# Scattering a sorted group three groups of gathers later, from three row buffers

## What is computed

```python
msgs = x[src]                                   # a row for each edge
dense = zeros((n + 1, 5, d)).at[dst_s, slot].set(msgs[order])
filled = dense[:, :4] + (~mask)[..., None] * (W @ blank + b)
srt = jnp.sort(filled, axis=1)                  # 4 values for each node and feature
out = jnp.einsum('nmd,m->nd', srt, cw) + cb
h = batch_norm(a * x + out[:-1], g, be)         # needs mean and variance over all nodes
x = x + h
```

## Time and profile before

| | us |
|---|---|
| median of three runs | 5594.01 |
| lowest, highest | 5585.44, 5599.05 |
| profiled execution, all of it | 5594.62 |
| its span, from first to last instruction | 5592.8 |

### The profile page before, as it was taken

The page is one execution under the profiler, slowest core; times in us unless marked ns, Lnnn a source line. Parts: engine busy times, 40 slices in busy tenths (PEclk is TensorE's granted clock), DMA queues, the critical chain, the costliest instruction groups (busy, mean ns, idle before and its releaser), DMA issues. The chain is left out here.

```text
span 5592.8 us, 61115 instructions
## 1 busy us (share of the span) xinstructions
PE 4068.6 (73%) x14728; PEld 2251.4 (40%) x14728; DVE 3828.8 (68%) x7518; ACT 2782.3 (50%) x5374; POOL 3409.5 (61%) x3399
## 2 busy tenths in 40 slices
PE   6755446700444775554879999999999989995597
PEld 4432223300222334442546555655565545553343
DVE  7876664588666358884768776877787778762276
ACT  6862222212222236664778645864685468544433
POOL 7757777776777727776777402730371057677677
PEclk9987668855766888887999999999999999997799
DMA  5643225876111589883768645864585467875455
GB/s 181 230 177 102 93 97 201 289 260 233 47 46 46 182 274 269 263 258 121 226 208 267 225 159 165 262 207 148 188 256 200 139 218 254 260 225 151 137 174 166
DMA packets 628092, 1062.85 MB, mean 190 GB/s; under 512 B 105048, under 2 KB 258158, under 8 KB 627740
## 3 DMA queue, kind: packets, MB, share of 16 engines
q1 hardware_dynamic: 498972, 818.46, 44.8%
q0 software_dynamic: 100544, 163.41, 10.5%
q10 hardware_dynamic: 28224, 77.08, 3.5%
HBM read 599.34 MB, written 464.81 MB: 190 GB/s over the span
## 5 line engine op out<-in xcount | busy, mean ns | idle before, releaser
L1831 POOL DMA_INDIRECT r_G<-msg_tab,srow x784 | 739.9, 944 | 1107.3 <-issue 1103.1
L827 PE MATMUL l_ps<-cv_V,cv_cwi 128*128 128x448 f32 x896 | 476.0, 699 | 815.6 <-DVEq L814 815.6
L827 PEld LDWEIGHTS l_ps<-cv_V,cv_cwi 128*128 128x128 f32 x896 | 218.8, 252 | 1073.4 <-issue 552.6
L1221 POOL DMA_INDIRECT x_tab<-a_r,node_pos x392 | 379.7, 969 | 223.6 <-issue 114.0
L2080 DVE TENSOR_TENSOR agg<-r_psS,agg 128x128 f32 x980 | 281.7, 287 | 289.8 <-PE r_psS L1938 216.7
L696 POOL DMA_INDIRECT o_tab<-cv_ob,put_idx x392 | 387.9, 989 | 148.7 <-issue 113.9
L1912 PE MATMUL r_psR<-r_hin,whh 128*128 128x512 f32 x882 | 453.4, 596 | 0.9 <-ACT r_ohn L2011 0.9
L688 POOL DMA_INDIRECT cv_M<-h_tab,gat_src x392 | 373.9, 954 | 119.4 <-issue 119.1
L1863 PEld LDWEIGHTS r_psM<-wmsg,r_hnew 128*128 128x128 f32 x2744 | 360.5, 192 | 169.7 <-issue 140.2
L1938 PE MATMUL r_psS<-r_sel,r_G 128*128 128x128 f32 x1960 | 293.8, 297 | 136.0 <-DMA r_G<-msg_tab,srow 135.0
L1863 PE MATMUL r_psM<-wmsg,r_hnew 128*128 128x128 f32 x2744 | 362.8, 275 | 3.9 <-DVE r_hnew L2144 3.9
(11 more groups left out here) (287 smaller groups left out, 10768.5 us busy)
## 6 DMA issues: line engine op xcount, KB each, us to landing
r_hin<-ht_tab SPq DMA_DIRECT2D x441, 256.0 KB
msg_tab<-r_m SPq DMA_DIRECT2D x392, 256.0 KB
ht_tab<-r_hnew SPq DMA_DIRECT2D x343, 256.0 KB
o_tab<-o_blank SPq DMA_DIRECT2D x98, 512.0 KB, 4.9
st_h<-h_tab SPq DMA_DIRECT2D x98, 512.0 KB, 3.7
st_o<-o_tab SPq DMA_DIRECT2D x98, 512.0 KB, 4.7
r_oin<-ht_tab SPq DMA_DIRECT2D x161, 256.0 KB
i_x<-x_tab SPq DMA_DIRECT2D x49, 528.0 KB
```

The source lines that it names most:

```text
L827: ins = nc.tensor.matmul(psO[:, h, 0:HW], cwi[m][:], V[i % 2][m][:, HW * h:HW * (h + 1)], start=m == 0, stop=m == 3)
L1221: pool.indirect_dma_start(x2_tab, bass.IndirectOffsetOnAxis(ap=node_pos[:, j:j + 1], axis=0), rb[i % RR][:, t, :], None).then_inc(s_out[i ...
L1831: pool.indirect_dma_start(G[g % GR][:, q, :], None, msg_tab[s % 3] if s else first_tab, bass.IndirectOffsetOnAxis(ap=at, axis=0)).then_inc ...
```

## The change

GpSimd's order in the sort of both layers becomes gather(0) to gather(3), scatter(0), gather(4), scatter(1), ... gather(27), scatter(24), scatter(25), scatter(26), scatter(27). The number of row buffers `ob` and of the semaphores that go with them becomes OR = 3, so that ACT's `rows(i)` waits for the scatter of group i - 3. SP's wait for the end of all scatters has three semaphores. The number of instructions that move data stays.

```diff
--- before.py
+++ after.py
@@ -36,6 +36,7 @@
 SR = 4
 AR = 3
 RR = 4
+OR = 3
 SW = P
 IDW = D + 4
 LNEPS = 1e-5
@@ -643,14 +644,14 @@
             s_srt = stage_sem(n + "sorted")
             s_mix = stage_sem(n + "mixed")
             s_o = stage_sem(n + "rows")
-            s_sc = [stage_sem(n + "put0"), stage_sem(n + "put1")]
+            s_sc = [stage_sem(f"{n}put{i}") for i in range(OR)]
             M0 = sb(n + "M_first", [P, 3, D], F32, c)
             M = [sb(f"{n}M{i}", [P, JC + 1, D], F32, c) for i in range(CR)]
             low = [sb(f"{n}low{i}", [P, JC + 2, D], F32, c) for i in range(2)]
             high = [sb(f"{n}high{i}", [P, JC + 2, D], F32, c) for i in range(2)]
             A = sb(n + "A", [P, JC, D], F32, c)
             V = [[sb(f"{n}V{i}{m}", [P, JC * D], F32, c) for m in range(4)] for i in range(2)]
-            ob = [sb(f"{n}ob{i}", [P, JC, D], F32, c) for i in range(2)]
+            ob = [sb(f"{n}ob{i}", [P, JC, D], F32, c) for i in range(OR)]
             cwi = [sb(f"{n}cwi{m}", [P, P], F32, c) for m in range(4)]
             HW = JC * D // 2
             psS, psL, psH, psW = banks
@@ -675,8 +676,8 @@
                 sp.wait_ge(s_fill, 16 * NCH)
 
             def scattered(sp):
-                for par in range(2):
-                    sp.wait_ge(s_sc[par], 16 * JC * (NC // 2))
+                for q in range(OR):
+                    sp.wait_ge(s_sc[q], 16 * JC * ((NC - 1 - q) // OR + 1))
 
             def gpsimd(pool):
                 def gather(i):
@@ -695,18 +696,18 @@
                         j = JC * i + q
                         pool.indirect_dma_start(o_tab[layer],
                                                 bass.IndirectOffsetOnAxis(ap=put_idx[:, j:j + 1], axis=0),
-                                                ob[i % 2][:, q, :], None, bounds_check=N - 1, oob_is_err=False
-                                                ).then_inc(s_sc[i % 2], 16)
+                                                ob[i % OR][:, q, :], None, bounds_check=N - 1, oob_is_err=False
+                                                ).then_inc(s_sc[i % OR], 16)
 
                 for q in range(3):
                     pool.indirect_dma_start(M0[:, q, :], None, h_tab[layer],
                                             bass.IndirectOffsetOnAxis(ap=gat_src[:, q:q + 1], axis=0)
                                             ).then_inc(s_m0, 16)
-                for i in range(NC + 2):
+                for i in range(NC + OR):
                     if i < NC:
                         gather(i)
-                    if i >= 2:
-                        scatter(i - 2)
+                    if i >= OR:
+                        scatter(i - OR)
 
             def scalar(act):
                 bl = blank_p[layer][:].unsqueeze(1)
@@ -746,9 +747,9 @@
 
                 def rows(i):
                     act.wait_ge(s_mix, i + 1)
-                    if i >= 2:
-                        act.wait_ge(s_sc[i % 2], 16 * JC * (i // 2))
-                    nc.scalar.activation(ob[i % 2][:].rearrange("p j f -> p (j f)").rearrange("p (h n) -> p h n", n=HW),
+                    if i >= OR:
+                        act.wait_ge(s_sc[i % OR], 16 * JC * (i // OR))
+                    nc.scalar.activation(ob[i % OR][:].rearrange("p j f -> p (j f)").rearrange("p (h n) -> p h n", n=HW),
                                          psO[:, :, 0:HW], ACT.Identity, bias=cbb[layer][:, 0:1]).then_inc(s_o, 1)
 
                 blank_first(-1)
```

## The result

| | before | after |
|---|---|---|
| median, us (7 runs each) | 5596.28 | 5566.32 |
| lowest, highest | 5585.44, 5599.15 | 5557.86, 5572.98 |
| profiled execution's span | 5592.8 | 5567.4 |
| ratio, 95% interval | | 0.9946 [0.9936, 0.9956] |

The change is worth 30 us of 5596, with an interval of 25 to 36. Forecast were 5568 and 26.1 less. It is clear of the 0.3% that one can tell from no change.

A forecast was written before the change was run, and what follows sets the result against it. GpSimd's issuing of gathers and scatters was taken as the bound, with idle holes at both ends of each sort. 8.80 + 5.48 + 6.09 + 5.71 = 26.1 us less gave a median of 5568, range 5557 to 5583.

The forecast's parts named there:

- (1): Sort heads: a fourth group of gathers fills the wait before the first scatter; gain 8.80 us layer 0, 6.09 layer 1.
- (2): Sort tails: three groups of scatters cover the wait for the last rows; gain 5.48 us layer 0, 5.71 layer 1.
- (3): Sort's middle: same instructions, scatters one group later, 0 us; ACT's wait for a scatter's landing has 10 us of cover.
- (4): Small parts: SP's third semaphore wait and one more semaphore cleared per stage; under 0.2 us, taken as 0.
- (5): Moved gathers beside DVE's sorting might take longer, costing up to 10 us; taken as 0.
- rival C: Holes filled, but something that doesn't move sets the end of the sort stages: no gain, 5594 us; chance 0.10.
- Rival D: Recurrent stage, 2913 to 5050: PE's granted clock falls; gain gone from 0.979 downward, 5635 us at 0.96; chance 0.05.
- Rival B: Only the heads' gain comes, last rows being late or gathers stretched: 14.9 us, time 5579; chance 0.09.

The follow-up runs named there:

- head alone: Changed kernel with four groups of gathers before the first scatter, but its last gathers left where they stood before the change: 5576.25 us, ratio 0.9955 to the kernel before.
- buffers alone: Changed kernel with three row buffers and semaphores kept, but scatters two groups behind the gathers as before: 5594.04 us, ratio 0.9993 to the kernel before.
- the change again: The changed kernel unaltered, rerun beside the kernel before on the same chip: 5563.97 us, ratio 0.9941.
- tail alone: Changed kernel with the old order up to group 25, then the last two gathers together and four scatters behind: 5587.89 us, ratio 0.9977 to the kernel before.
- lag one: Changed kernel with scatters one group behind the gathers, three buffers: 6535 us (before 6451), ratio 1.037, and 6446 us (before 6453) in three sets.
- deeper lags: Changed kernel with lag three and two buffers (ratios 1.013, 1.004), lag four and three buffers (1.0045), or unaltered (1.0059), against the kernel before.

## Why the prediction was right

**(1) The head.** Forecast a hole of 3.6 us in layer 0 and none in layer 1, gain 8.80 + 6.09. Measured 3.61 and 0.30; head alone shortened the sorts by 9.04 and 6.33.

**(2) The tail.** Forecast 5.48 + 5.71, rows ready 3.3 and 3.1 us early. Measured waits of 0.30, and the tail alone gave 5.67 and 5.26. In after the slack in layer 0 is 880.64 less the eviction's end at 876.69 and the 0.77 that GpSimd took to follow one: 3.2 us.

**(3) The middle and the buffers.** Forecast 0; buffers alone gave +0.9 us in the trace and a ratio that includes 1. ACT's evictions in after waited for PE only (394.3 us over 56), so the cover of 10 us sufficed, with landings of at most 4.3 us, and 7.4 in the change again. Landings later than that were not seen in the two.

**(4), (5) Small parts, longer gathers.** Nothing to be seen: the pause at the border is 4.21 us, where it was 4.43, and the mean gather 953 ns.

**What follows.** The sum of 26.1 us was for the sorts, and they gave 26.3, and 27.5 in the change again. The 30 of the medians has an interval of 25 to 36, which takes 26.3 in; whether anything beyond the sorts belongs to the change isn't shown. In the profiled execution layer 1 started 18.25 us earlier, where 14.4 were from the sort: 3.9 came from the look-ups between, the landmark that I had put at 1346.6 and that came at 1342.59. So the first row behind the sort of layer 1, put at 1850.5, came at 1846.40, while the first look-up came at 889.64, where 889.7 was forecast. Behind the sort of layer 1 the execution lost 4.8 us (last column of the table, within its scatter), so that its span shrank by 25.4. That span and sum agree within 0.7 us is therefore partly luck, 3.9 against 4.8. But nothing behind the sorts swallowed a shift of this size, as the waits of the earlier trace rows had said: rival C is out. Rival D is out too, for these runs: the granted clock from 2913 to 5050 is 0.99 in after as in the earlier trace rows. (Its bound comes out at 0.978 and not 0.979: 2137 us at 0.99 grow by 26 us at 0.978.) Rival B needed a wait before the last scatters, and there is none.

The rule of the Trainium skill's Perfetto Trace Analysis (What "DMA-bound" means) that large descriptors are what matters for a solid issuing sequencer (the "only" of the prediction is not in it) fits the middle here in so far as the new order gained nothing there; larger descriptors were not tried. It would have given 0 for the whole. What the order won lay in the 30 us in which the sequencer wasn't solid, 26 of which are now filled.

## What to carry to other kernels

Where an engine's in-order issuing is the bound, look at the two ends of its loop: a work item's latency through the other engines (23.9 us here from its last gather to its first scatter, and 30.0 for the very first group of layer 0, from 394.56 to 424.59) against the issuing that the lag puts in between: at the tail 18.1 us with two groups of scatters and 27.2 with three, at the head 17.6 with two groups of gathers and 26.4 with three. The middle looks saturated with either lag; the ends pay the difference once each, and a lag so short that what it puts in between in the middle (17.9 us with lag one) is less than the latency pays in every group. Price the hole row by row, keep the first ready time fixed, and check that what follows the loop starts at its last item. Here the sum for the sorts was good to 1.4 us, and the scatter of the runs was the larger part of the error.

## What was not expected of the hardware

**Look-ups beside the statistics.** In the six traces of the first table the stretch from the first look-up to the border of layer 1 took 452.8 to 453.6 us in the three kernels with a filled head (after, again, head alone), and 456.8 to 458.0 in the three without. The look-ups themselves make the difference, 211.4 to 213.8 us busy in the one case and 216.0 to 218.7 in the other; DVE waits for them, 16.4 to 17.4 us in the one and 20.4 to 21.1 in the other. A look-up takes 0.94 us by itself, and up to 2.0 beside a DVE addition with both operands in SBUF; the pair in the earlier trace rows is 1.93 beside such an addition of 1.28. Not each one is stretched: in before 65 of the 196 look-ups overlap such an addition, and 38 of these take more than 1.2 us, while most of the others keep to 0.94; without an addition none is longer than 1.2. The three with a filled head have 30 to 35 stretched ones, the others 38 to 40. The Trainium skill, SBUF — State Buffer, section Who interferes with whom, has it that such an operation contends with a GpSimd instruction that reads SBUF; the pair of rows agrees, and so do the gathers of the sort, beside operations with one operand in PSUM, at 0.94. Why a filled head should shift the two against each other by 4 us wasn't tried, and three traces against three may be chance: in the later sets lag one, with its head open, has 211.5 us of look-ups twice.

**Conditions in which the change shows no gain.** In the three sets at 6440 us the deeper lags had evictions held up for up to 33 us, behind a signal of PE that came 25 us after its last matmul, and GpSimd's queue was no longer dense. The same kernel was worth 0.9941 in the first set and 1.0059 [0.9994, 1.0123] in the last. A gain of 0.5% holds for the conditions in which it was measured.
